# State-space layers of a fused kernel: normalisation through centring products in the output stage, coefficients on GpSimd, tokens of two blocks placed by ScalarE

## The reference, cut to what matters

```python
def _layernorm_channels(z, w, b):
    mu = mean(z, channels); var = mean((z - mu) ** 2, channels)
    return (z - mu) * rsqrt(var + 1e-05) * w + b
def _s4d_layer(z, ...):
    dtA = (-exp(A_re_log) + 1j * A_im) * exp(log_dt)
    C = (C_re + 1j * C_im) * expm1(dtA) / A
    K = 2 * real(sum over 32 modes of C * exp(dtA * l))    # one kernel per channel
    y = gelu(causal_convolution(z, K) + z * D_skip)
    out = W @ y + b
    return out[:128] * sigmoid(out[128:])
for i in range(4):
    h = _s4d_layer(_layernorm_channels(h, ln_w[i], ln_b[i]), ...) + h
```

## Time and profile before

| | |
|---|---|
| runs | 1318.26, 1323.85, 1315.74 us; median 1318.26 |
| profiled execution | 1325.82 us, span 1324.0 us |
| mean granted TensorE clock | 0.847 |
| busy in the span | PE 996.8 us (75%), DVE 819.0 (62%), ACT 518.8 (39%), POOL 379.3 (29%) |
| DMA | 76.55 MB, mean 58 GB/s |
| chain that ended last | PE 48%, DVE 20%, POOL 12%, ACT 10%, issue 7%, DMA 3% |

### The profile page before, as it was taken

One profiled execution on the slowest core, in us unless ns is written; L12 is line 12 of the kernel. 1 busy time (PEld: TensorE's weight loads), 2 busy tenths in 40 slices (PEclk: granted clock), 3 DMA queues, 4 the chain that ended last, 5 costly groups with the idle time before them and its releaser, 6 DMA issues.

```text
span 1324.0 us, 20100 instructions
## 1 busy us (share of the span) xinstructions
PE 996.8 (75%) x7756; PEld 672.0 (51%) x7756; DVE 819.0 (62%) x1570; ACT 518.8 (39%) x1228; POOL 379.3 (29%) x356
## 2 busy tenths in 40 slices
PE   5484774847344389999999768769799688979877
PEld 3272442625323267878787533235466434456543
DVE  1589777797747434646464588679555438945443
ACT  1654463543123221312121330047687225767622
POOL 0140404104006500000000325449544407934310
PEclk9875866858676589999999779879799798979868
...
DMA packets 60450, 76.55 MB, mean 58 GB/s; under 512 B 37464, under 2 KB 41956, under 8 KB 58596
## 3 DMA queue, kind: packets, MB, share of 16 engines
...
...
## 4 chain that ended last, share of the span: by engine, by line
PE 48%; DVE 20%; POOL 12%; ACT 10%; issue 7%; DMA 3%; SPq 1%; DVEq 0%; POOLq 0%; ACTq 0%
PE psum L992 7%; PE psum L994 6%; PE psum L993 6%; POOL rest L1222 3%; ACT rest L1175 3%; POOL rest L1212 3%; POOL rest L1218 2%; PE psum L1410 2%; PE psum L670 2%; PE psum L642 2%; ACT main L747 2%; PE psum L1477 2%; PE psum L1419 2%; PE psum L1478 2%; PE psum L1463 2%
## 5 line engine op out<-in xcount | busy, mean ns | idle before, releaser
L402 POOL TENSOR_TENSOR kept<-kept 128x8 f32<-128x8 f32 x20 | 4.0, 202 | 488.5 <-DVE kept L379 488.5
L1175 ACT ACTIVATE rest<-psum,main 128x128 f32<-128x128 f32 x256 | 113.4, 480 | 12.3 <-POOL main L1233 10.7
L839 ACT ACTIVATE x_high<-main 128x512 fp32r<-128x512 f32 x48 | 30.3, 633 | 199.6 <-DVE main L913 199.6
L992 PE MATMUL psum<-x_high,w_low 128*128 128x512 f32 x192 | 77.3, 403 | 19.6 <-DVE x_low L918 19.6
L658 PE MATMUL psum<-main 128*32 128x64 f32 x1024 | 23.6, 278 | 79.6 <-DMA main<-main 79.1
L416 ACT ACTIVATE main<-psum,kept 128x128 f32<-128x128 f32 x40 | 14.5, 471 | 169.1 <-POOL kept L409 169.1
L1241 POOL TENSOR_TENSOR rest<-rest,main 128x512 f32<-128x512 f32 x64 | 65.4, 1043 | 47.3 <-DVE main L1306 47.3
L993 PE MATMUL psum<-x_low,w_high 128*128 128x512 f32 x192 | 76.7, 400 | 0.0
L994 PE MATMUL psum<-x_high,w_high 128*128 128x512 f32 x192 | 76.6, 399 | 0.0
L992 PE MATMUL psum<-hid_high,w_low 128*128 128x512 f32 x192 | 75.6, 394 | 0.7 <-DVE main L937 0.7
L913 DVE TENSOR_TENSOR main<-kept,rest 128x512 f32<-128x512 f32 x48 | 33.0, 690 | 68.8 <-PE psum L994 44.6
...
## 6 DMA issues: line engine op xcount, KB each, us to landing
...
```

The costliest lines, as they stand in the source:

```text
L992: T.matmul(dst, w_small, x_large, start=first, stop=False)
L1175: last = A.activation(probs[:, p, 4 * r + m, :], bank[2 * p + r][:, m * P:(m + 1) * P], ACT.Exp, scale=row_scale[:, c, r, m:m + 1], bias=r ...
```

## The change

- **Normalisation.** Per block, TensorE multiplies hT by a centring matrix (identity minus 1/128) in bank 0; ScalarE squares the result; TensorE multiplies the square by a column of 1/128, which gives the variance of each token; VectorE adds epsilon, GpSimd takes the power -1/2. A second product of hT with the centring matrix weighted by the layer's weights (`weighted`, made by GpSimd) gives centred and weighted tokens in bank 2; VectorE scales and adds the bias. For blocks 0 and 1 it writes rows (`z_rows`) and ScalarE copies them into the strided places of `zu`; for blocks 2 and 3 it writes them there itself. The first centring product stands between the gated products of blocks 2 and 3 of the layer before.
- **Turned-back powers.** They use two banks in place of four. Six groups stand before the gated products, the others between the centring steps.
- **Kernel products and what hangs on them.** They stand behind the chunk inputs and far angles, and so do ScalarE's copies and SyncE's writes to DRAM and Toeplitz copies.
- **Coefficients.** They go from VectorE to GpSimd, whose order in a layer is decay, `weighted`, coefficients, phases, with the first two powers -1/2 between the phase sums. VectorE keeps the reciprocal (`s4_dve_inverse`). Parameters are double and loaded two layers ahead.
- **ScalarE's tables.** Three one-column activations per layer (`warm`) load the sine, Gelu and sigmoid tables ahead of the waits.
- **Last layer.** The gated sum into xT follows each block rather than all four.

```diff
-        def s4_dve_powers(dve, chain, G, mag):
+        def s4_dve_powers(dve, G, mag):
...
+            dve.wait_ge(sem("s4_mag"), G + 1)
+            V.tensor_copy(small[12], pow_re[:, :, FIRST])
+            V.tensor_copy(small[13], mag[:, :, FIRST]).then_inc(sem("s4_pow"), 1)
+            dve.wait_ge(sem("s4_pow"), G * 3 + 1)
+            V.tensor_tensor(pow_im, pow_im, mag, ALU.mult).then_inc(sem("s4_pow"), 1)
+            V.scalar_tensor_tensor(pow_re, pow_re, 1.0, mag, ALU.subtract, ALU.mult, reverse0=True).then_inc(sem("s4_pow"), 1)
+        def s4_dve_eps(dve, N, b):
+            dve.wait_ge(sem("s4_var"), N * BLOCKS + b + 1)
+            nc.vector.tensor_scalar(var_eps[:, 4 * b:4 * b + 4], bank[CENTRED][:, 0:4], EPS_LN, None, ALU.add).then_inc(sem("s4_var_eps"), 1)
+        def s4_dve_z(dve, N, b):
+            tokens = zu[0:CHUNK].rearrange("p h (t half) -> p half t h", half=2)
+            dve.wait_ge(sem("s4_rstd"), N * BLOCKS + b + 1)
+            dve.wait_ge(sem("s4_z_ps"), N * BLOCKS + b + 1)
+            for t in range(4):
+                for half in range(2):
+                    r = slice(CHUNK * half, CHUNK * half + CHUNK)
+                    last = nc.vector.scalar_tensor_tensor(tokens[:, half, 4 * b + t, :], bank[SCORED][r, t * P:(t + 1) * P],
+                                                          rstd[r, 4 * b + t:4 * b + t + 1], ln_wb[r, 1, :], ALU.mult, ALU.add)
+            last.then_inc(sem("s4_z"), 1)
+        def s4_dve_z_rows(dve, N, b):
+            dve.wait_ge(sem("s4_rstd"), N * BLOCKS + b + 1)
+            dve.wait_ge(sem("s4_z_ps"), N * BLOCKS + b + 1)
+            for t in range(4):
+                c = 4 * b + t
+                last = nc.vector.scalar_tensor_tensor(z_rows[b][:, t, :], bank[SCORED][:, t * P:(t + 1) * P],
+                                                      rstd[:, c:c + 1], ln_wb[:, 1, :], ALU.mult, ALU.add)
+            last.then_inc(sem("s4_z_rows"), 1)
...
         def s4_dve_layer(dve, chain, L, more):
             V = nc.vector
             link = chain.link
             if more:
...
+            if L + 2 < S4_LAYERS:
+                s4_dve_inverse(link, L + 2)
             if more:
-                s4_dve_powers(dve, chain, L + 1, near(LOW_BANKS))
+                s4_dve_powers(dve, L + 1, near(LOW_BANKS))
             dve.wait_ge(sem("s4_y"), L * PIECES + PIECES)
             V.transpose(yT.rearrange("p (c i) -> p i c", i=CHUNK), y_act).then_inc(sem("s4_yT"), 1)
...
-            for b in range(BLOCKS):
-                dve.wait_ge(sem("s4_sig"), L * BLOCKS + b + 1)
...
+            if more:
+                for b in range(3):
+                    s4_dve_glu(dve, link, L, b)
+                s4_dve_eps(dve, L + 1, 0)
+                s4_dve_glu(dve, link, L, 3)
+                for b in range(BLOCKS):
+                    if b < BLOCKS - 1:
+                        s4_dve_eps(dve, L + 1, b + 1)
+                    (s4_dve_z_rows if b < 2 else s4_dve_z)(dve, L + 1, b)
+            else:
+                for b in range(BLOCKS):
+                    s4_dve_glu(dve, link, L, b)
+                    sl = slice(512 * b, 512 * b + 512)
+                    dve.wait_ge(sem("s4_h"), L * BLOCKS + b + 1)
+                    V.scalar_tensor_tensor(xT[:, sl], hT[:, sl], gate[:, 2:3], xT[:, sl], ALU.mult, ALU.add).then_inc(sem("x_s4"), 1)
...
-        def s4_pe_layer(pe, L, first, more):
+        def s4_pe_back(pe, N, groups):
+            for q in groups:
+                if q >= 2:
+                    pe.wait_ge(sem("s4_back"), N * BACKS + q - 1)
+                for i in range(4):
+                    last = nc.tensor.transpose(bank[TURNED_BACK[q % 2]][0:CHUNK, i * P:(i + 1) * P], (pow_re, pow_im)[i % 2][:, 2 * q + i // 2, :], ident)
+                last.then_inc(sem("s4_back_ps"), 1)
+        def s4_pe_centre(pe, N, b):
+            if N:
+                pe.wait_ge(sem("s4_h"), (N - 1) * BLOCKS + b + 1)
+            if b:
+                pe.wait_ge(sem("s4_var_eps"), N * BLOCKS + b)
+            nc.tensor.matmul(bank[CENTRED][:, :], centre, hT[:, 512 * b:512 * b + 512], start=True, stop=True).then_inc(sem("s4_centred"), 1)
+        def s4_pe_var(pe, N, b):
+            pe.wait_ge(sem("s4_sq"), N * BLOCKS + b + 1)
+            for t in range(4):
+                last = nc.tensor.matmul(bank[CENTRED][:, t:t + 1], h_sq[b % 2][:, t * P:(t + 1) * P], mean_col, start=True, stop=True)
+            last.then_inc(sem("s4_var"), 1)
+        def s4_pe_z(pe, N, b):
+            if b:
+                pe.wait_ge(sem("s4_z_rows"), N * 2 + b) if b <= 2 else pe.wait_ge(sem("s4_z"), N * 2 + 1)
+            else:
+                pe.wait_ge(sem("s4_weighted"), N + 1)
+            for t in range(4):
+                c = 4 * b + t
+                last = nc.tensor.matmul(bank[SCORED][:, t * P:(t + 1) * P], hT[:, c * P:(c + 1) * P], weighted, start=True, stop=True)
+            last.then_inc(sem("s4_z_ps"), 1)
...
+        def s4_pe_layer(pe, L, more):
...
-                    last = T.transpose(bank[4 + q % 4][0:CHUNK, i * P:(i + 1) * P], (pow_re, pow_im)[i % 2][:, 2 * q + i // 2, :], ident)
-                last.then_inc(sem("s4_back_ps"), 1)
...
+            if L:
+                pe.wait_ge(sem("s4_h"), L * BLOCKS)
             if more:
                 s4_pe_near_angles(pe, L + 1)
-            pe.wait_ge(sem("s4_z"), L + 1)
+            pe.wait_ge(sem("s4_back"), (L + 1) * BACKS)
+            pe.wait_ge(sem("s4_z"), (L + 1) * 2)
+            pe.wait_ge(sem("s4_z_act"), (L + 1) * 2)
             for k in range(PIECES):
                 for hh in range(PIECE * k, PIECE * (k + 1)):
...
+                q, at = hh // PIECE, CHUNK * (hh % PIECE)
+                dst = bank[6][32 * q:32 * q + GROUPS, at:at + CHUNK]
+                T.matmul(dst, sel_re[:, hh, :], pow_re[:, hh, :], start=True, stop=False)
+                last = T.matmul(dst, sel_im[:, hh, :], pow_im[:, hh, :], start=False, stop=True)
+            last.then_inc(sem("s4_k_ps"), 1)
+            pe.wait_ge(sem("s4_ln_in"), L * 32 + 32)
+            for q in range(PIECES):
+                dst, hs = bank[7][32 * q:32 * q + GROUPS, 0:PIECE], slice(PIECE * q, PIECE * (q + 1))
+                T.matmul(dst, sel[:, 0, :], small[8][:, hs], start=True, stop=False)
+                last = T.matmul(dst, ident[0:GROUPS, 0:GROUPS], skip[:, hs], start=False, stop=True)
...
+            pe.wait_ge(sem("s4_k_rows"), (L + 1) * 2)
             pe.wait_ge(sem("s4_toep_in"), L * 16 * PIECES + 16 * PIECES)
             pe.wait_ge(sem("s4_pow_moved"), L * 128 + 128)
             pe.wait_ge(sem("s4_u_moved"), L * 128 + 128)
...
             pe.wait_ge(sem("s4_y_ps"), (L + 1) * PIECES)
             pe.sem_inc(sem("s4_tp_free"), 1)
+            if more:
+                pe.wait_ge(sem("s4_pow"), (L + 2) * 3)
+                if L + 2 < S4_LAYERS:
+                    s4_pe_dta(pe, L + 2, CENTRED)
+                s4_pe_back(pe, L + 1, range(EARLY))
...
+            pe.wait_ge(sem("s4_glu_in"), L * 32 + 32)
+            for b in range(3 if more else BLOCKS):
+                s4_pe_glu(pe, L, b)
+            if not more:
+                return
+            if L + 2 < S4_LAYERS:
+                pe.wait_ge(sem("s4_dtaT"), L + 3)
+            s4_pe_centre(pe, L + 1, 0)
+            s4_pe_glu(pe, L, 3)
+            s4_pe_var(pe, L + 1, 0)
+            s4_pe_z(pe, L + 1, 0)
+            for b in range(1, BLOCKS):
+                s4_pe_centre(pe, L + 1, b)
+                s4_pe_back(pe, L + 1, range(EARLY + 2 * (b - 1), EARLY + 2 * b))
+                s4_pe_var(pe, L + 1, b)
+            for b in range(1, BLOCKS):
+                s4_pe_z(pe, L + 1, b)
+                if b == 1:
+                    s4_pe_back(pe, L + 1, range(EARLY + 6, BACKS))
...
+        def s4_act_square(act, N, b):
+            act.wait_ge(sem("s4_centred"), N * BLOCKS + b + 1)
+            nc.scalar.activation(h_sq[b % 2], bank[CENTRED][:, :], ACT.Square).then_inc(sem("s4_sq"), 1)
+        def s4_act_z(act, N, b):
+            tokens = zu[0:CHUNK].rearrange("p h (t half) -> p half t h", half=2)
+            act.wait_ge(sem("s4_z_rows"), N * 2 + b + 1)
+            for half in range(2):
+                r = slice(CHUNK * half, CHUNK * half + CHUNK)
+                last = nc.scalar.activation(tokens[:, half, 4 * b:4 * b + 4, :], z_rows[b][r], ACT.Copy)
+            last.then_inc(sem("s4_z_act"), 1)
...
+        def s4_act_layer(act, L, more):
+            A = nc.scalar
             if more:
                 s4_act_round_near(act, L + 1)
+            if L + 2 < S4_LAYERS:
+                s4_act_rates(act, L + 2)
+            if more:
+                s4_act_round_far(act, L + 1)
+                A.activation(warm[:, 3 * L + 1:3 * L + 2], warm[:, 0:1], ACT.Sin)
+            s4_act_k_rows(act, L)
+            if more:
                 s4_act_sines_near(act, L + 1)
-                s4_act_round_far(act, L + 1)
                 s4_act_sines_far(act, L + 1)
```

(77 more changed lines are left out.)

407 lines of the change are left out of this document (184 added, 223 removed).

## The result

| | before | after |
|---|---|---|
| median of the runs | 1320.8 us (4 runs) | 1370.6 us (1368.3 to 1382.4, 4 runs) |
| ratio | | 1.040, 95% interval 1.033 to 1.047 |
| profiled span | 1324.0 us | 1366.5 us |
| state-space part ends at | 397.9 us | 447.2 us |

The forecast was 1335 us, range 1305 to 1355: the sign was right, the size was not. The state-space part grew by 49.3 us, as the medians did (49.7).

The account below looks back on a forecast made before the run. VectorE was taken to bound Stage A (then state copies) and Stage C. Terms +2.2 +2.2 +26.7 -6.0 -3.5 -4.7 gave +16.9 us on the median of 1318.3: 1335 us, range 1305 to 1355.

Parts of the forecast that it names:

- Stage A: First chunk-input product to first output product: late kernel products put the Toeplitz chain on the path, +26.7 us over four layers.
- Rivals 1 and 2: Stage A at its lower bound, 1317 us, chance 0.24; Toeplitz matrix still in under VectorE's chain, 1300 us, chance 0.15.
- Stage C: Normalisation, last write of hT to next chunk inputs: becomes a four-engine chain hardly shorter, -3.5 us in all.
- the tail of its chain: End of Stage C: z products 0.9 us each, copies 1.8, powers 1.5, strided pieces 2.6, near angles 4.0.
- a sign of being wrong: Stage C under 18 or over 27 us would show the prediction wrong.
- waits of this length did not lower: Argument against Rival 3: the old Stage C kept clock 0.84 to 0.99 with TensorE busy 20 of 23 us.
- Rival 3: TensorE falls to 1.2 GHz in Stage C, making means and z products dearer: +21 us, 1356 us, chance 0.17.
- Stage B: First output product to last write of hT: sigmoid load off the chain, warm first products, -2 per layer, -6 us.
- hidden: In Stage B, GpSimd's coefficients and phases, estimated 16 us, stay behind output products, transpose and gates, 20 us.
- Start: Up to the first chunk inputs: normalisation rounds, sines, power products, powers, near angles; 95.8 us instead of 93.6, +2.2.
- The first near rounding's wait: Layer 0's first near rounding waits for GpSimd's phases: another +2.2 us, called the loosest number.
- End: Last stretch: both table loads off the chain, -2.6, three of four residual adds into gaps, -2.1: -4.7 us.

Follow-up runs that it names:

- e1: Changed kernel plus seven unused TensorE products filling its two waits in each output stage: 1358.8 us, ratio 1.028.
- e12: Changed kernel with GpSimd's six wide phase products behind the four reciprocal roots instead of around them: 1367.2 us, ratio 1.033.
- e11: Changed kernel with z as whole rows, the start reordered, and every layer's kernel products ahead of the far angles: 1327.2 us, ratio 1.004.
- e8: Changed kernel with all four blocks of z written as whole rows and copied into place by ScalarE: 1356.0 us, ratio 1.024.
- e7: Changed kernel with kernel products of layers 1 to 3 in the output stage before, layer 0's ahead of its far angles: 1333.3 us, ratio 1.006.

## Why the prediction was wrong

- **Stage A was right in its mechanism and nearly in its size.** Predicted 41.9, measured 42.5 in layers 1 and 2; 36.4 against 39.0 in layer 3. Products took 8.4 us (8.9 taken), copies 3.1, DRAM 2.5 (2.6), Toeplitz and state copies 17.5 (16.6). Layer 3's inputs ran at 1.2 GHz throughout (7.05 us, 5.2 taken), which is most of its miss. Rivals 1 and 2 fall with this.
- **Stage C is the step that failed**: -3.5 predicted, +14.5 measured, 18 of the 32 us missed. The term that failed is the tail of its chain, the last powers, z products and near angles, priced at full clock throughout; two of the three stages came out over the 27 us that I had named as a sign of being wrong. Its first part held: from the second centring product to the first of the last z products 9.3 us predicted, 9.2 measured. The tail did not. I wrote that "waits of this length did not lower" the clock, arguing from a stage whose waits were short and whose mean was high; the tail has waits of 3.0 and 3.7 us. Behind them powers, z products and near angles cost up to twice their price: 4.1, 5.5 and 0.8 us in the three transitions by e1, 10.4 of the 18. The rest is work priced too low, 2.0, 2.0 and 3.5 us: in the transition after layer 1 the strided pieces took 0.44 us each, not 0.33 (+0.9), copies 1.06, not 0.9 (+0.3), products 1.1, not 0.9; the last transition has both blocks of strided pieces on its path. The terms as I listed them also add up to 23.0, not 23.2 us, which makes the miss 0.2 us larger each time.
- **Rival 3 named the cause and placed it wrongly.** It put 1.2 GHz on the one-column means and z products of every block (1356 us). The rounds stayed at 2.4 GHz; it was the end of the stage that fell, the last z products and above all the near angles, a term that the rival did not hold. I gave it 0.17. Its +21 us beside a measured 10.4 us for the clock is no hit either.
- **Stage B**: -6 predicted, -1.2 measured. Both pieces of the term were real (no table load between transpose and gate; warm first products), but ScalarE's six groups of powers now stand ahead of the gate, with the table load ahead of them on the chain (1.28 us at 244.7, behind the Gelu), and the additions meet GpSimd's phases (1.10 to 1.64 us instead of 0.69; e12). That GpSimd is "hidden" was argued by end times only; what it does to its neighbour while it runs was left out.
- **Start**: +2.2 predicted, +5.9 in this profile, 5 to 8 by the count from the first turns: ScalarE's order of copies, table load and sines. The first near rounding's wait, +2.2 without a sum behind it, shows: it starts when GpSimd's last phase sum ends, and layer 0's stage A is 1.5 us longer than layer 1's. **End**: -4.7 predicted, -2.5 measured.

What stays open: why the same wait of 3.0 us kept the clock in some transitions and lost it in others, why the near angles fell behind a wait of 1.3 us in e11 and not in e8, and in e7 without any; and how the start's remaining 3 us split.
